# Routing stage of a hybrid-attention kernel: feature products in two row groups, six unit banks, and the first half's gates and weighted paths inside the stage

## The reference, cut to what matters

```python
outs = [local_out, mid_out, delta_out, v_direct]          # each (B, L, H=4, dh=64)
feats = [mean and variance of each o_, and mean of each product outs[i]*outs[j]]   # 14 per head
router_feat = concatenate([hidden_states] + feats)        # 256 + 56 columns
h1 = silu(router_feat @ r_w1 + r_b1)                      # 312 -> 624
logits = (h1 @ r_w2 + r_b2).reshape(B, L, H, 4)
p = softmax(logits) * (1.0 - 4.0 * FLOOR) + FLOOR
mixed = sum(p[..., i:i+1] * outs[i] for i in range(4))
# then two rms norms over dh and the product with Wo
```

## Time and profile before

| what | value |
|---|---|
| median of 3 runs | 8044.31 us (8039.78 to 8051.16) |
| the profiled execution | 8032.48 us |
| its span | 8030.8 us |
| TensorE busy | 7292.0 us, 91% of the span |
| VectorE, ScalarE, GpSimd busy | 4779.2, 3394.8, 1780.1 us |
| mean granted TensorE clock | 0.965 |

### The profile page before, as it was taken

The page is one execution under the profiler, slowest core; times in us unless marked ns, Lnnn a source line. Parts: engine busy times, 40 slices in busy tenths (PEclk is TensorE's granted clock), DMA queues, the critical chain, the costliest instruction groups (busy, mean ns, idle before and its releaser), DMA issues. The chain is left out here.

```text
span 8030.8 us, 122663 instructions
## 1 busy us (share of the span) xinstructions
PE 7292.0 (91%) x47742; PEld 4230.0 (53%) x47902; DVE 4779.2 (60%) x9348; ACT 3394.8 (42%) x6915; POOL 1780.1 (22%) x2690
## 2 busy tenths in 40 slices
PE   6999998999989999999999999999999999999999
PEld 3646455464554645546465464654645546455464
DVE  5565655656656566564665646656566665656546
ACT  3352543525436253352533525345253452534425
POOL 2212222122211222112221122212212122122221
PEclk9999999999999999999999999999999999999999
DMA  3011221212112021120221202222022220212102
GB/s 75 19 32 31 38 42 22 34 25 38 42 24 44 14 38 42 30 41 16 33 42 30 41 15 33 43 38 43 6 33 43 38 43 6 34 42 38 43 8 36
DMA packets 337771, 268.59 MB, mean 33 GB/s; under 512 B 213521, under 2 KB 276369, under 8 KB 337097
## 3 DMA queue, kind: packets, MB, share of 16 engines
q1 hardware_dynamic: 337148, 260.09, 17.1%
HBM read 48.71 MB, written 42.02 MB: 11 GB/s over the span
## 5 line engine op out<-in xcount | busy, mean ns | idle before, releaser
L1928 ACT ACTIVATE pre<-ps 128x512 f32<-128x512 f32 (+3 forms) x3072 | 1274.8, 493 | 737.2 <-PE ps L1916 731.9
L1853 DVE TENSOR_REDUCE sa_nm<-ps 128x2 f32<-128x1024 f32 (+4 forms) x1280 | 1390.6, 1115 | 290.3 <-PE ps L1834 138.1
L1916 PE MATMUL ps<-sa_qs,sa_ks 99*128 99x512 bf16 (+3 forms) x3072 | 801.9, 335 | 79.4 <-ACT pre L1928 58.5
L1935 POOL TENSOR_SCALAR_AFFINE_SELECT pre<-pre 128x512 f32<-128x512 f32 x512 | 325.9, 637 | 1711.1 <-ACT pre L1928 1708.5
L1834 PE MATMUL ps<-sa_ks,sa_qs 96*128 96x512 bf16 (+3 forms) x2560 | 638.8, 324 | 51.7 <-DVE sa_nm L1853 34.3
L1948 PE MATMUL ps<-pre,sa_va 128*17 128x512 f32 (+3 forms) x6144 | 645.6, 492 | 8.2 <-POOL pre L1935 8.2
L1916 PEld LDWEIGHTS ps<-sa_qs,sa_ks 99*128 99x128 bf16 x3072 | 258.8, 98 | 658.2 <-ACT pre L1928 474.3
L716 PE MATMUL ps<-rep,stack 128*32 128x512 f32 x4608 | 515.9, 598 | 8.6 <-DMA rep<-paths 8.4
L330 PE MATMUL ps<-identb 128*128 128x512 bf16 x1856 | 466.1, 394 | 22.8 <-ACT dr_z L1168 10.5
L962 POOL TENSOR_TENSOR A<-paths 128x256 f32<-128x256 f32 x384 | 268.1, 726 | 778.5 <-DVE paths L1134 778.5
L1834 PEld LDWEIGHTS ps<-sa_ks,sa_qs 96*128 96x128 bf16 x2560 | 243.7, 99 | 234.9 <-DVE sa_nm L1853 69.0
(11 more groups left out here) (370 smaller groups left out, 14083.3 us busy)
## 6 DMA issues: line engine op xcount, KB each, us to landing
sa_qs<-sa_parts SPq DMA_DIRECT2D x288, 128.0 KB, 4.8
sa_ks<-sa_parts SPq DMA_DIRECT2D x288, 128.0 KB, 5.9
x<-in_x SPq DMA_DIRECT2D x17, 1024.0 KB, 5.6
rep<-paths SPq DMA_DIRECT2D x128, 128.0 KB, 2.4
bounce<-paths SPq DMA_DIRECT2D x32, 512.0 KB, 2.9
out_y<-x SPq DMA_DIRECT2D x32, 512.0 KB, 3.0
rep<-paths SPq DMA_DIRECT2D x128, 127.9 KB, 3.1
rep<-paths SPq DMA_DIRECT2D x128, 127.8 KB, 3.1
```

The lines of the kernel that those rows point to most:

```text
L1853: nc.vector.tensor_reduce(nm[:, g % 2, op.c, op.t, op.j:op.j + op.heads], cols, AX.X, ALU.max, negate=True).then_inc(s.slot_free, 1)
L1916: last = nc.tensor.matmul(bank[:, off:], ks[0:QROWS, g % NBUF, j, kt * P:(kt + 1) * P], qs[0:QROWS, g % NBUF, j, n * BANK + off:(n + 1) * ...
L1928: nc.scalar.activation(pt[:, gs % 2, j, off:BANK], ring_bank(ring_use(gs, j))[:, off:], ACT.Exp, scale=RATIO).then_inc(s.ring_out, 1)
L1935: nc.gpsimd.affine_select(block, block, [[0, GH], [1, P]], ALU.is_ge, 0.0, base=0, channel_multiplier=-1).then_inc(s.masked, 1)
```

## The change

- The routing weights of the features are loaded a second time, to partitions 64 to 119 of `k.rw1`. VectorE copies the 56 finished feature columns to columns 64 to 119 of the same buffer (`both`); the transposes and the copies to `FT` are 120 wide instead of 56.
- `from_features(u)` issues the feature products of units u and u + 1 together, the even one on rows 0 to 55, the odd one on rows 64 to 119. Each keeps its wait for `FT` and its signal.
- The units use six banks in turn; partial logits go to banks 0 and 1, the logits to bank 6.
- TensorE's order is written out anew: four units' hidden products ahead of the transposes instead of three, and the rest as in the diff. The partial logits wait for each chunk by itself, where they waited for all five.
- Logits, maximum, exponential and gates are done for each half by itself. Between the halves, after units 5 to 7, ScalarE does the first half's exponential, then units 8 and 9, then the second half's. VectorE weights three paths of the first half after its gates, and the fourth after the copy of the second half's partial logits. The next stage weights the second half's four paths alone, and its first mix waits for no path.
- Ten `keep_warm` products stand at the end of the stage on TensorE.
- A semaphore `read` is added: it orders VectorE's own read of the logits, and the second gather's write of that bank.

```diff
+SIDE = P // 2
...
                     (k.rw1[0:FEATS, 2, :], w["rw1"][D:D + FEATS]),
+                    (k.rw1[SIDE:SIDE + FEATS, 2, :], w["rw1"][D:D + FEATS]),
...
-PARTIAL = (7, 0)
+PARTIAL = (0, 1)
+UNIT_BANKS = (2, 3, 4, 5, 6, 7)
+LOGITS, SPARE = 6, 7
+
+
+def weigh_path(nc, m, i, n):
+
+    tn, gn = T // NB, T * H // NB
+    path = (m.local_tm, m.mid_tm, m.delta_tm, m.v_tm)[i][:, n * tn:(n + 1) * tn, :].rearrange("p t (h d) -> p (t h) d", h=H)
+    return nc.vector.tensor_tensor(path, path, m.prob[:, n * gn:(n + 1) * gn, i:i + 1].to_broadcast([P, gn, DH]), ALU.mult)
...
-        F = m.feats
+        F, both = m.feats, k.xn[:, :, 0:SIDE + FEATS]
...
-        FT = sb("ro_ft", [FEATS, L])
+        FT = sb("ro_ft", [SIDE + FEATS, L])
...
+                def exponentials(n):
+                    act.wait_ge(s.shifted, n + 1)
+                    nc.scalar.activation(lg[:, groups(n), :], lg[:, groups(n), :], ACT.Exp).then_inc(s.exp, 1)
+
                 for n in range(NB):
                     act.wait_ge(s.ft_ps, n + 1)
-                    nc.scalar.activation(FT[:, n * BANK:(n + 1) * BANK], ps[0:FEATS, n, :], ACT.Copy).then_inc(s.ft, 1)
...
+                    nc.scalar.activation(FT[:, n * BANK:(n + 1) * BANK], ps[0:SIDE + FEATS, n, :], ACT.Copy).then_inc(s.ft, 1)
+                for u in range(HC + 3):
+                    hidden(u)
+                exponentials(0)
+                for u in range(HC + 3, NB * HC):
+                    hidden(u)
+                exponentials(1)
...
-                last.then_inc(s.feats, 1)
+                settle(last)
+                nc.vector.tensor_copy(both[:, :, SIDE:SIDE + FEATS], F).then_inc(s.feats, 1)
 
                 for n in range(NB):
+                    tiles, half = slice(n * (BANK // P), (n + 1) * (BANK // P)), groups(n)
                     dve.wait_ge(s.partial_ps, n + 1)
                     nc.vector.tensor_copy(partial[:, n * BANK:(n + 1) * BANK], ps[:, PARTIAL[n], :]).then_inc(s.partial, 1)
...
+                    if n:
+                        weigh_path(nc, m, PATHS - 1, 0)
+                    dve.wait_ge(s.logits, n + 1)
...
+                    gates = nc.vector.tensor_scalar(m.prob[:, half, :], lg[:, half, :], 1.0 - PATHS * FLOOR, FLOOR, ALU.mult, ALU.add)
+                    if n == 0:
+                        settle(gates)
+                        for i in range(PATHS - 1):
+                            weigh_path(nc, m, i, 0)
...
                 def from_hidden(u):
                     n, cols, out, hid = unit(u)
-                    if u >= 4:
-                        pe.wait_ge(s.h1, u - 3)
+                    if u >= len(UNIT_BANKS):
+                        pe.wait_ge(s.h1, u - len(UNIT_BANKS) + 1)
...
+                def from_features(u):
+                    for v in (u, u + 1):
+                        n, cols, out, hid = unit(v)
+                        rows = slice(SIDE * (v % 2), SIDE * (v % 2) + FEATS)
+                        pe.wait_ge(s.ft, n + 1)
+                        nc.tensor.matmul(out, k.rw1[rows, 2, hid], FT[rows, cols], start=False, stop=True).then_inc(s.h1_ps, 1)
+
                 def partial_logits_of(n):
-                    pe.wait_ge(s.h1, (n + 1) * HC)
                     for c in range(HC):
+                        pe.wait_ge(s.h1, n * HC + c + 1)
...
                 def gather_logits_of(n):
                     pe.wait_ge(s.partial, n + 1)
+                    if n:
+                        pe.wait_ge(s.read, n)
...
-                for u in range(3):
+                for u in range(4):
                     from_hidden(u)
                 pe.wait_ge(s.feats, 1)
...
-                for u in range(NB * HC):
-                    n, cols, out, hid = unit(u)
-                    pe.wait_ge(s.ft, n + 1)
-                    nc.tensor.matmul(out, k.rw1[0:FEATS, 2, hid], FT[:, cols], start=False, stop=True).then_inc(s.h1_ps, 1)
-                    if u + 3 < NB * HC:
-                        from_hidden(u + 3)
-                    if u == HC + 1:
-                        partial_logits_of(0)
+                from_hidden(4)
+                from_features(0)
+                from_features(2)
+                from_hidden(5)
+                from_features(4)
+                from_hidden(6)
+                partial_logits_of(0)
+                from_hidden(7)
+                from_features(6)
                 gather_logits_of(0)
+                from_hidden(8)
+                from_hidden(9)
+                from_features(8)
                 partial_logits_of(1)
-                gather_logits_of(1).then_inc(s.logits, 1)
+                gather_logits_of(1)
+                keep_warm(nc, k, ps[:, SPARE, :], 10)
...
-                for n in range(NB):
-                    for i in range(PATHS):
-                        nc.vector.tensor_tensor(of(paths[i], n), of(paths[i], n),
-                                                m.prob[:, n * GN:(n + 1) * GN, i:i + 1].to_broadcast([P, GN, DH]),
-                                                ALU.mult).then_inc(s.part, 1)
+                for i in range(PATHS):
+                    weigh_path(nc, m, i, 1).then_inc(s.part, 1)
...
-                        pe.wait_ge(s.part, PATHS * n + i + 1)
+                        if n:
+                            pe.wait_ge(s.part, i + 1)
...
-    "ro": "feats ft_ps ft h1_ps h1 partial_ps partial logits shifted exp",
+    "ro": "feats ft_ps ft h1_ps h1 partial_ps partial logits read shifted exp",
```

More of the change, by code:

```diff
@@ L1206, in route, with groups @@
         partial = sb("ro_partial", [P, L])
+        def groups(n):
+            return slice(n * (T * H // NB), (n + 1) * (T * H // NB))
         def feature(first, n):
@@ L1213, in _, with hidden @@
             def _(act):
+                def hidden(u):
+                    n, c = u // HC, u % HC
+                    rows = P if c < HC - 1 else HLAST
+                    act.wait_ge(s.h1_ps, u + 1)
+                    nc.scalar.activation(h1T[0:rows, c, n * BANK:(n + 1) * BANK], ps[0:rows, UNIT_BANKS[u % len(UNIT_BANKS)], :],
+                                         ACT.Silu, bias=k.rb1[0:rows, c:c + 1]).then_inc(s.h1, 1)
+                def exponentials(n):
+                    act.wait_ge(s.shifted, n + 1)
+                    nc.scalar.activation(lg[:, groups(n), :], lg[:, groups(n), :], ACT.Exp).then_inc(s.exp, 1)
                 for n in range(NB):
                     act.wait_ge(s.ft_ps, n + 1)
-                    nc.scalar.activation(FT[:, n * BANK:(n + 1) * BANK], ps[0:FEATS, n, :], ACT.Copy).then_inc(s.ft, 1)
-                for n in range(NB):
[L1218 to L1226, removed]
+                    nc.scalar.activation(FT[:, n * BANK:(n + 1) * BANK], ps[0:SIDE + FEATS, n, :], ACT.Copy).then_inc(s.ft, 1)
[5 more added lines that the diff above has]
+                exponentials(1)
             @block.vector
@@ new lines, in _ @@
+                    nc.vector.tensor_tensor(lg[:, half, :].rearrange("p (t h) c -> p t (h c)", h=H),
+                                            ps[:, LOGITS, 0:T * H * PATHS].rearrange("p (t n) -> p t n", t=T)[:, tiles],
+                                            k.rb2[:].unsqueeze(1).to_broadcast([P, BANK // P, H * PATHS]), ALU.add).then_inc(s.read, 1)
+                    dve.wait_ge(s.read, n + 1)
+                    settle(nc.vector.tensor_reduce(red[:, half], lg[:, half, :], AX.X, ALU.max))
@@ new lines, in _ @@
+                    nc.vector.tensor_tensor(lg[:, half, :], lg[:, half, :], bc(red[:, half], PATHS), ALU.subtract).then_inc(s.shifted, 1)
+                    dve.wait_ge(s.exp, n + 1)
+                    settle(nc.vector.tensor_reduce(red[:, half], lg[:, half, :], AX.X, ALU.add))
+                    settle(nc.vector.reciprocal(red[:, half], red[:, half]))
+                    settle(nc.vector.tensor_tensor(lg[:, half, :], lg[:, half, :], bc(red[:, half], PATHS), ALU.mult))
+                    gates = nc.vector.tensor_scalar(m.prob[:, half, :], lg[:, half, :], 1.0 - PATHS * FLOOR, FLOOR, ALU.mult, ALU.add)
@@ L1286, in gather_logits_of @@
                     pe.wait_ge(s.partial, n + 1)
+                    if n:
+                        pe.wait_ge(s.read, n)
                     for t in range(n * (BANK // P), (n + 1) * (BANK // P)):
-                        last = nc.tensor.matmul(ps[:, 6, t * H * PATHS:(t + 1) * H * PATHS], partial[:, t * P:(t + 1) * P],
+                        last = nc.tensor.matmul(ps[:, LOGITS, t * H * PATHS:(t + 1) * H * PATHS], partial[:, t * P:(t + 1) * P],
                                                 k.gather[:], start=(t == 0), stop=True, skip_group_check=True)
-                    return last
-                for u in range(3):
+                    last.then_inc(s.logits, 1)
+                for u in range(4):
                     from_hidden(u)
@@ L1296, in _ @@
                     for i in range(BANK // P):
```

(19 more changed lines are left out.)

5 lines of the change are left out of this document (2 added, 3 removed).

## The result

| | median | lowest to highest | runs |
|---|---|---|---|
| before | 8042.05 us | 8038.98 to 8051.16 | 4 |
| changed | 7858.7 us | 7827.22 to 7865.22 | 4 |

The ratio is 0.9762, interval [0.9738, 0.9786]: 2.4% faster, 183 us by the medians. I had forecast faster, and 7962 us with a range of 7906 to 8006. The sign was right.

What follows compares the result with a forecast made beforehand. TensorE was taken to bound the routing stage up to the last gather, then a VectorE and ScalarE chain. Gains of 4.3 + 0.8 = 5.1 us a sequence, 82 us in sixteen, gave 7962 us from the median, range 7906 to 8006.

Steps and rivals of the forecast that it cites:

- Where the time goes: Routing stage: TensorE sets the time up to the last gather, then small VectorE and ScalarE steps with TensorE idle.
- The pairing: Routing stage's feature products and first half's partial logits: records overlap only partly, 14 slots (6.0 us) and 6 (2.6 us).
- full pairs: Rival, chance 0.30: both records of paired products run side by side despite waits and signals, 2.6 us a sequence more, 7921 us.
- The tail: Routing stage's end after the second half's partial logits start: first mixing product at 779.6 instead of 783.86, 4.3 us a sequence.
- The half-size steps: Routing stage's end: three VectorE steps on half the logits take 0.26 us each, between 0.15 and 0.33.
- The table loads: ScalarE in the routing stage: two extra function table loads of 1.28 us each, hidden behind TensorE's work, costing nothing.
- The margin of 1.0 us for the three paths: VectorE in the routing stage: three paths weighted by 774.1, copy of partial logits due at 775.1, so no delay.
- The copy of 448 elements: VectorE's extra feature copy before the transposes: about 0.7 us with its wait, under 5 us of cover.
- One check that I named: Changed profile: the mixing stage's first product should start 31 us after the transposes, where it was 35.6.
- nine changes of row count: TensorE in the routing stage: nine switches between row counts, 1.8 us together in the sum.
- The clock: TensorE at the mixing stage's head: 0.8 us a sequence gained, between 1.55 gained and 1.7 lost.
- The range: Whole kernel: 7906 to 8006 us, said to leave out less than 2 in 10.

Runs made afterwards that it cites:

- experiment three: The kernel before with eighteen warming products added behind the last gather and nothing else; 8009.93 us, ratio 0.9961.
- four: The changed kernel without its ten warming products at the routing stage's end; 7898.6 us, ratio 0.983 to the kernel before.
- experiment eight: The changed kernel with 20 warming products instead of 10 at the delta rule's end, ahead of the routing stage; 7834.58 us, ratio 0.9735 to the kernel before.
- eleven: The kernel before with four warming products added in the middle of the routing stage; 8029.81 us, ratio 0.9977.
- twelve: The kernel before with eight warming products added in the middle of the routing stage; 8048.05 us, ratio 1.0015.
- six: The changed kernel with 18 warming products instead of 10 at the routing stage's end; 7880.17 us, ratio 0.9797 to the kernel before.
- seven: The changed kernel with 26 warming products instead of 10 at the routing stage's end; 7909.86 us, ratio 0.9831 to the kernel before.

## Why the prediction was wrong, point by point

*Where the time goes.* Right: the stage up to the last gather is TensorE's, and what comes after it is a chain of small steps.

*The pairing.* This step failed. I held that a signal in between must follow its own product's second record, and so took 14 slots instead of 10, and 6 for the partial logits instead of 4. The trace shows 10 and 4, with every wait and signal in place. The runs with all products on one row group and with the pairs alone (experiments one and two) show it too, at 0.43 us a slot. It cost the forecast 2.6 us a sequence, 41 us. The rows for full pairs were before me; I gave an argument about order more weight than two rows of the same thing.

*The tail.* With full pairs the sum gives 42.4 - 4.3 - 2.6 = 35.5 us from the routing stage's first product to the mixing stage's; measured 35.2 in the second sequence. The half-size steps took the 0.26 us I had taken (758.21 to 758.47 is one of them). The table loads were 1.28 us each, hidden, without any drain that shows: by the measurement 1.28 holds here, and not the 2.66 of the Trainium skill's "ScalarE: Activation LUTs", section "What ACT_TABLE_LOAD costs". The margin of 1.0 us for the three paths was 0.6. The copy of 448 elements took 0.4 us, not 0.7, and was hidden. One check that I named was ill put: unit 3's hidden products now stand ahead of the transposes, so the time from the transposes to the mixing stage is short by them. It was 26.7 us, against the 31 I had named; 31.3 less 2.6 for the pairs and 1.7 for unit 3 is 27.0. The sum also took nine changes of row count where the new order has eight, 0.2 us.

*The clock.* This term was mis-sized: 0.8 us a sequence, 13 us, with 1.55 as its upper end. At the mixing stage's head alone it was 2.0 us, 32 us in all (experiments three and four). I had read 3.1 us at half clock from one sequence; over sixteen, the head took 12.8 us and not that sequence's 12.3, and 10.8 at full clock. It also left two things out. In the kernel before every sequence paid for 3.4 us at half clock somewhere in the routing stage: at its head in nine, later in the others, which is why nearly all took 42.4 to 42.5 us all the same. In the changed kernel seven sequences don't pay in the first profile, two in the second. And outside both stretches the time at half clock fell from 382 and 393 us to 233 and 294. Of the gain, some 16 to 52 us lie there, by the closest and the farthest pair of profiles.

*The range.* It took both bounds of the pairing, but of the clock only one stage's. The best case, full pairs and best clock, was given as 7909; with 32 us at the head instead of 25 it is 7902. The other 43 us down to 7859 go with less time at half clock, inside the routing stage (some 17 us by the profiles' means) and outside of both stretches (34). No experiment changed the clock outside alone, so for that part this is read from the profiles and not shown. With the pairing taken right the forecast was the rival's 7921, and the remaining 62 us are this term: 19 at the mixing stage's head (16 x 1.2) and these 43.

*What stays open.* That the rest of the kernel runs at full clock more often is seen in the profiles. Inside the routing stage, experiment eight shows that products ahead of its head decide it there, and the profiles of eleven and twelve point the same way for its end. What decides it outside is not settled: on the changed kernel experiments six and seven show no dependence on length in the times, and the 25 us of experiment three that its profile does not show are of the same kind.

## What to carry to other kernels

Products of 56 rows on two row groups ran fully side by side in float32, even with a semaphore wait ahead of each and a signal behind each (1.99 us for eight records, 3.70 on one row group); so such a contraction is worth a second copy of its weights where TensorE sets the time. Behind a stage that ends in a chain of small VectorE and ScalarE steps, look at the granted clock of the next stage's first microseconds in all repetitions: a few warming products that end before the chain does gave 2.0 to 2.2 us a sequence, and those too many cost about their full length (experiments three, six and seven). A forecast for a kernel whose clock changes often should keep a term for the clock outside the changed stage: here, stages that nobody touched moved by 0.2 to 0.6% of the kernel's time.

## What was not expected of the hardware

- An idle time of 2.39 us behind narrow products (16 columns moving) was followed by half clock in sixteen of sixteen sequences; ten bf16 products of 512 columns in the same place, 2.2 us, kept full clock in sixteen of sixteen. Ahead of the routing stage nearly the same idle time, 2.38 us, stands behind such bf16 products, and half clock followed in nine and fourteen of sixteen sequences. So the length of the idle time alone did not decide it.
- The kernel before became no slower when 14 us of idle products were added to it: 8 us faster by the medians, ratio 0.9977 [0.9955, 0.9999]. In six of sixteen sequences 3.4 us at half clock in the same stage were gone with them.
- An activation table load is issued before the wait of the activation that needs it, and that activation follows it within 0.02 us (758.49 + 1.28, 759.78). The three loads in a stage lay beside other engines' work and cost nothing on the path.
